# Experts as sorted token tiles, and four blocks as one stream of heads

## The reference

```
qp, kp = exp(q.W - |q|^2/2), exp(k.W - |k|^2/2)         # 16 heads of 64, 128 features
S_t = S_(t-1) + k_t v_t^T ;  a_t = (q_t.S_t) / (q_t.sum k + eps)     # causal linear attention
x1 = layernorm(x + a @ Wo)
x2 = layernorm(x1 + differential cross attention over the context)   # 32 half heads of 8
s = sigmoid(x2 @ gate_w.T)                               # 16 experts in 4 groups
best 2 groups, then best 4 experts of them; w = 2.5 * s / sum of the chosen s
out = layernorm(x2 + shared(x2) + sum_k w_k * expert_k(x2))
expert(x) = (silu(x @ gate.T) * (x @ up.T)) @ down.T     # 256 -> 128 -> 256
```

## Time and profile before

| | us |
|---|---|
| median of 3 runs | 1121.97 |
| span of the profiled execution (the time it has) | 1123.0 |
| TensorE busy | 957.9 (85%) |
| VectorE busy | 684.9 (61%) |
| ScalarE busy | 511.6 (46%) |
| GpSimd busy | 290.7 (26%) |
| moved by DMA | 81.72 MB, 73 GB/s |

### The profile page before, as it was taken

How to read it: one execution, slowest core, us unless ns; L and a number is a source line. 1 busy time by engine, 2 the same in 40 slices (tenths; PEclk the granted TensorE clock), 3 DMA queues, 4 the chain that set the end, 5 groups by cost and what they waited for, 6 DMA issues and landing times.

```text
span 1123.0 us, 20741 instructions
## 1 busy us (share of the span) xinstructions
PE 957.9 (85%) x7032; PEld 664.1 (59%) x7032; DVE 684.9 (61%) x1834; ACT 511.6 (46%) x910; POOL 290.7 (26%) x297
## 2 busy tenths in 40 slices
PE   4899976789998899789998899789998899764896
PEld 1477765347777566347777665347777675333453
DVE  5576643455556866654556766655556767855756
ACT  4676620367772323357773223347773223253221
POOL 2211100024440112125441112214441122133222
PEclk9999977799998999899998999989999999866998
DMA  5655652211113123201113123311114122300231
GB/s 158 214 163 160 129 123 80 67 29 30 39 29 104 57 71 93 80 19 39 30 39 104 52 64 89 89 26 37 32 29 113 43 65 87 94 1 1 73 106 52
DMA packets 79134, 81.72 MB, mean 73 GB/s; under 512 B 17968, under 2 KB 62640, under 8 KB 79024
## 3 DMA queue, kind: packets, MB, share of 16 engines
q1 hardware_dynamic: 79024, 80.31, 26.4%
HBM read 48.62 MB, written 11.73 MB: 54 GB/s over the span
## 4 chain that ended last, share of the span: by engine, by line
PE 64%; ACT 14%; DVE 11%; issue 6%; DMA 2%; POOL 1%; SPq 1%; DVEq 0%; ACTq 0%; POOLq 0%
PE ps_a L1171 18%; PE ps_xo L1171 6%; PE ps_o L1198 5%; PE ps_o L1197 4%; PE ps_o L1171 3%; PE ps_f L1171 3%; PE ps_turn L1171 3%; PE ps_att L1313 3%; PE ps_st L1326 3%; PE ps_st L1171 2%; PE ps_att L1171 2%; ACT square L690 2%; PE ps_f L1302 2%; ACT qk L685 2%; ACT qk L684 2%
## 5 line engine op out<-in xcount | busy, mean ns | idle before, releaser
L605 POOL TENSOR_TENSOR hT<-square,qk 128x512 f16<-128x512 f32 x64 | 74.0, 1157 | 370.8 <-DVE qk L935 370.8
L639 POOL TENSOR_TENSOR hT<-ffn_mem,hT 128x512 f16<-128x512 f32 x68 | 83.5, 1229 | 315.6 <-ACT hT L773 315.6
L933 DVE SCALAR_TENSOR_TENSOR hT<-ps_a,qk 128x512 f16<-128x512 f32 x64 | 44.3, 692 | 169.9 <-ACT square L690 165.5
L619 POOL TENSOR_TENSOR prob<-ffn_mem,prob 128x512 f16<-128x512 f32 x84 | 97.1, 1156 | 87.7 <-ACT ffn_mem L731 87.7
L1171 PE MATMUL ps_a<-turned,ffn_mem 128*128 128x512 f16 x432 | 101.3, 385 | 0.5 <-DMA ffn_mem<-ffn_split 0.5
L1198 PE MATMUL ps_o<-run,qf 128*128 128x65 f32 x480 | 93.8, 277 | 0.0
L1197 PE MATMUL ps_o<-v,att 128*128 128x65 f32 x480 | 90.4, 270 | 0.0
L1197 PEld LDWEIGHTS ps_o<-v,att 128*128 128x128 f32 x480 | 77.8, 194 | 7.7 <-issue 0.3
L1302 PE MATMUL ps_f<-qk,w_feat_high 128*128 128x512 f16 x128 | 48.9, 382 | 34.9 <-ACT qf L712 25.6
L1171 PE MATMUL ps_a<-w_v,x_split 128*128 128x512 f16 x192 | 54.4, 439 | 25.4 <-DVE w_v L823 12.9
L1326 PEld LDWEIGHTS ps_st<-v,kt 128*128 128x128 f32 x512 | 70.1, 200 | 8.3 <-ACT kt L708 0.3
(11 more groups left out here) (235 smaller groups left out, 2162.9 us busy)
## 6 DMA issues: line engine op xcount, KB each, us to landing
ffn_mem<-ffn_split SPq DMA_DIRECT2D x68, 256.0 KB, 3.0
qk<-hT SPq DMA_DIRECT2D x128, 128.0 KB, 2.4
ffn_mem<-ffn_split SPq DMA_DIRECT2D x68, 128.0 KB, 2.5
ffn_mem<-ffn_w SPq DMA_DIRECT2D x17, 384.0 KB, 4.3
ffn_split<-ffn_mem SPq DMA_DIRECT2D x17, 384.0 KB, 2.5
xv<-xv_blocks SPq DMA_DIRECT2D x4, 816.0 KB, 5.9
xq<-xq_hl SPq DMA_DIRECT2D x48, 64.0 KB, 2.0
x_stage<-xT SPq DMA_DIRECT2D x5, 512.0 KB, 5.1
```

The costliest lines, as they stand in the source:

```text
L605: pool.tensor_tensor(low_parts[:, n % 2, 1, :], square[:, n % 2, :], qk[:, n % 2, n // 2 % 2, 0, 1, :], ALU.subtract).then_inc(p_sql.sem, 1)
L619: pool.tensor_tensor(prob[:, n % RING, 1, :], prob_full[:, n % 2, :], prob[:, n % RING, 0, :], ALU.subtract).then_inc(pr_low[n % 2].sem, 1)
L639: pool.tensor_tensor(hT[:, e % 3, 1, :], hid[:, e % 2, :], hT[:, e % 3, 0, :], ALU.subtract).then_inc(h_low.sem, 1)
L933: dve.scalar_tensor_tensor(low_parts[:, n % 2, 0, :], bank[:, :], 1 / W_SCALE, pair[:, 0, 0, :], ALU.mult, ALU.subtract).then_inc(p_low.se ...
```

## The change

- The program is one list of jobs, `schedule()`, that every engine walks without a loop. The heads of the four blocks follow one another (64 steps and four to drain), with the values of block b in the steps around its first head, and the chain of each block (output projection to token sorting) spread over the steps 4 to 20 after its attention.
- Each job that writes PSUM takes the next of eight banks in rotation.
- In even blocks the running state starts from zero, and the first chunk's product with it is left out; in odd blocks the state after the last chunk is not made.
- Only the shared expert is dense. For the others a prefix sum over the chosen experts gives every token and choice a row in a DRAM buffer sorted by expert; 16 indirect DMAs of 128 rows on GpSimd's queue write a block's rows. Blocks 0 to 2 are group 0, block 3 is group 1. Tiles of 128 rows (64 and 32 of them, two to a pair) are read from a row number held in a register, multiplied with the weights of the expert held in another register (all weights are in SBUF, in the memory of the attention weights), and stored. For each block 16 indirect DMAs fetch the rows back, and VectorE accumulates them with their weights (`combine`).
- SyncE writes 128 rows of zeros behind the last row of each expert (`table`).
- Silu is made from Tanh. A probability tile has one exponential; VectorE makes its fp16 copy.
- Setup weights have staging memory of their own.

The job lists, whole:

```diff
-            with pe.Fori(0, NBLK - 1) as i:
-                shared(i + 1, i)
-                ffn(i, i + 1)
+GROUPS = ((0, 1, 2), (3,))
+NGRP = len(GROUPS)
+GROUP_OF = {b: g for g, blocks in enumerate(GROUPS) for b in blocks}
+TOKENS = [len(blocks) * TB for blocks in GROUPS]
+REGION = [t + P for t in TOKENS]
+TILES = [2 * -(-(t * TOPK // P + NE - 1) // 2) for t in TOKENS]
+PAIRS_OF = [t // 2 for t in TILES]
+SPARE = [t - n * TOPK // P for t, n in zip(TILES, TOKENS)]
+ROWS = [NE * r + s * P for r, s in zip(REGION, SPARE)]
+TILE_BASE = [sum(TILES[:g]) for g in range(NGRP)]
+PAIR_BASE = [sum(PAIRS_OF[:g]) for g in range(NGRP)]
+XG = 3
+YG = 4
...
+def attention_jobs(t):
+    jobs = []
+    def add(kind, g, per):
+        if 0 <= g < NBLK * per:
+            jobs.append((kind, g // per, g % per))
+    if t + 2 >= 2:
+        add("project", t + 2, H)
+    add("turn keys", t - 1, H)
+    add("q features", t, H)
+    add("state", t - 2, H)
+    add("attend", t - 1, H)
+    if t % 2 == 1:
+        add("turn output", (t - 5) // 2, PAIRS)
+    add("k features", t, H)
+    add("output", t - 3, H)
+    for b in range(1, NBLK):
+        for c in range(NT):
+            if t == H * b - NT + c:
+                jobs.insert(3, ("values", b, 2 * c))
+            if t == H * b + NT - 1 + c:
+                jobs.insert(3, ("values", b, 2 * c + 1))
+    return jobs
+def weighs(b, last_chunk):
+    return [("weigh", b, m) for g in range(NG) if last_chunk == GC * g + GC - 1 for m in (2 * g, 2 * g + 1)]
+def chain_jobs(b, s):
+    def several(kind, ns):
+        return [(kind, b, n) for n in ns]
+    jobs = []
+    if s == 4:
+        jobs += several("project out", range(NT)) + [("norm1", b, 0)]
+    if s == 5:
+        jobs += several("turn stream", range(2))
+    if s == 6:
+        jobs += several("queries", range(KD))
+    if s in (7, 8, 9):
+        jobs += several("scores", {7: range(0, 6), 8: range(6, 19), 9: range(19, 32)}[s])
+    if s == 10:
+        jobs += several("turn maxima", [0])
+    if 11 <= s <= 15:
+        for n in range(6 * (s - 11), min(6 * (s - 10), CHUNKS) + 0):
+            jobs += [("probs", b, n)]
+            if n >= 3:
+                jobs += weighs(b, n - 3)
+        if s == 15:
+            jobs += weighs(b, CHUNKS - 1) + [("norm2", b, 0)]
+    if s == 16:
+        jobs += several("turn cross", range(2))
+    if s == 17:
+        jobs += several("gate", [0]) + several("route", [0]) + several("shared up", range(2)) + several("route", [1])
+    if s == 18:
+        jobs += several("route", [2]) + several("shared down", range(2))
+    if s == 19:
+        jobs += several("route", [3]) + several("prefix", [0])
+    if s == 20:
+        jobs += several("dispatch", [0]) + several("keep", [0])
+        if b == GROUPS[GROUP_OF[b]][-1]:
+            jobs += [("table", GROUP_OF[b], 0)]
+    return jobs
+def merged(main, extra):
+    out, done = [], 0
+    for i, job in enumerate(main):
+        out.append(job)
+        upto = len(extra) * (i + 1) // len(main)
+        out += extra[done:upto]
+        done = upto
+    return out + extra[done:]
...
+def tile_jobs(grp, s):
+    n, jobs = PAIRS_OF[grp], []
+    for kind, k in (("rows in", s + 2), ("tile turn", s), ("tile up", s - 1), ("tile turn back", s - 2),
+                    ("tile down", s - 3), ("rows out", s - 3)):
+        if 0 <= k < n:
+            jobs.append((kind, grp, k))
+    return jobs
...
+def schedule():
+    jobs = [("values", 0, n) for n in range(2 * NT)]
+    jobs += [("project", 0, 0), ("project", 0, 1), ("context", 0, 0)]
+    last = H * NBLK + 4
+    for t in range(last):
+        extra = []
+        for b in range(NBLK):
+            if t == H * b + 1 and b + 1 < NBLK:
+                extra.append(("load x", b + 1, 0))
+            if b and t == H * b - 6:
+                extra.append(("split x", b, 0))
+            if t == H * b + 13:
+                extra.append(("load stream", b, 0))
+            if t == H * b + 1 + H and b % BLK_PER_BATCH == 0:
+                extra.append(("load context", b, 0))
+            extra += chain_jobs(b, t - H * (b + 1))
+        jobs += merged(attention_jobs(t), extra)
+        if t < EXPERTS + 1:
+            jobs.append(("setup", 0, t))
+        if t == H * NBLK - 8:
+            jobs.append(("experts", 0, 0))
+        if t == H * NBLK - 1:
+            jobs.append(("experts", 0, 1))
+    b = NBLK - 1
+    chain = []
+    for s in range(4, 21):
+        chain.append(chain_jobs(b, s))
+    jobs += chain_jobs(NBLK - 2, last - H * (NBLK - 1))
+    jobs += chain[0]
+    gaps = {1: chain[1], 2: chain[2]}
+    scores = [j for part in chain[3:6] for j in part]
+    for i in range(7):
+        gaps[4 + i] = scores[5 * i:5 * i + 5]
+    gaps[12] = chain[6]
+    weigh = [j for part in chain[7:12] for j in part]
+    per = -(-len(weigh) // 12)
+    for i in range(12):
+        gaps[14 + i] = weigh[per * i:per * (i + 1)]
+    for i, part in enumerate(chain[12:]):
+        gaps[28 + i] = part
+    for s in range(-2, PAIRS_OF[0] + 4):
+        jobs += merged(tile_jobs(0, s) or [("none", 0, 0)], gaps.pop(s, []))
+    for s in sorted(gaps):
+        jobs += gaps[s]
+    first = [(bb, c) for bb in GROUPS[0] for c in range(NT)]
+    for s in range(-2, PAIRS_OF[1] + 4):
+        extra = []
+        if 0 <= s < len(first):
+            bb, c = first[s]
+            if c == 0:
+                extra.append(("load sum", bb, 0))
+            extra.append(("gather", bb, c))
+        if 1 <= s <= len(first):
+            bb, c = first[s - 1]
+            extra.append(("combine", bb, c))
+            if c == NT - 1:
+                extra.append(("norm3", bb, 0))
+        jobs += merged(tile_jobs(1, s) or [("none", 0, 0)], extra)
+    for bb in GROUPS[-1]:
+        if bb != b:
+            jobs.append(("load sum", bb, 0))
+        for c in range(NT):
+            jobs.append(("gather", bb, c))
+        for c in range(NT):
+            jobs.append(("combine", bb, c))
+        jobs.append(("norm3", bb, 0))
+    return jobs
...
```

The bodies that matter, in the order SyncE, GpSimd, ScalarE, VectorE, TensorE:

```diff
-ps_a = [psum("ps_a0"), psum("ps_a1")]
+banks = [stack.enter_context(nc.psum_tensor(f"ps{i}", [P, 512], F32)) for i in range(8)]
+KEY_BANK, VALUE_BANK = 6, 7
+BANK = {}
+turn = 0
+early = True
+for kind, b, n in SCHEDULE:
+    if kind == "q features" and (b, n) == (0, 4):
+        early = False
+    if kind in ON_PSUM and job_bank(kind, b, n) not in BANK:
+        if early and turn % 8 in (KEY_BANK, VALUE_BANK):
+            turn += 8 - turn % 8
+        BANK[job_bank(kind, b, n)] = turn % 8
+        turn += 1
...
+        elif kind == "table":
+            sp.wait_ge(*table_ready(0, b + 1))
+            for e in range(NE):
+                r = sp.value_load(end_i[0:1, b, e:e + 1], min_val=0, max_val=ROWS[b] - P)
+                sp.dma_start(rows_in[b][bass.ds(r, P), :], zero_row[:, :]).then_inc(ends_zeroed[b].sem, 16)
+        elif kind == "rows in":
+            i = pair_id(b, n)
+            if n == 0:
+                for bb in GROUPS[b]:
+                    sp.wait_ge(*scattered[bb](0, NT * TOPK))
+                sp.wait_ge(*ends_zeroed[b](0, NE))
...
+            if i >= XG:
+                sp.wait_ge(*t_turned(0, i - XG + 1))
+            for j in range(2):
+                t = TILE_BASE[b] + 2 * n + j
+                r = sp.value_load(row_i[0:1, t:t + 1], min_val=0, max_val=ROWS[b] - P)
+                sp.dma_start(xg[:, i % XG, j, :], rows_in[b][bass.ds(r, P), :]
+                             ).then_inc(xg_loaded[i % XG].sem, 16)
+        elif kind == "rows out":
+            i = pair_id(b, n)
+            sp.wait_ge(*t_kept(0, i + 1))
+            tiles = rows_out[b][2 * P * n:2 * P * (n + 1), :].rearrange("(j p) d -> p j d", p=P)
+            sp.dma_start(tiles, yb[:, i % XG, :, :]).then_inc(yb_stored[i % XG].sem, 16)
...
+        elif kind == "dispatch":
+            pool.wait_ge(*slots_ready(b, 1))
+            for j in range(NT * TOPK):
+                pool.indirect_dma_start(
+                    rows_in[GROUP_OF[b]], bass.IndirectOffsetOnAxis(ap=slot_i[:, b, j:j + 1], axis=0),
+                    stream[:, b % 2, j // TOPK, :], None).then_inc(scattered[b].sem, 16)
+        elif kind == "gather":
+            i = NT * b + n
+            if n == 0 and b == GROUPS[GROUP_OF[b]][0]:
+                upto_pair = PAIR_BASE[GROUP_OF[b]] + PAIRS_OF[GROUP_OF[b]]
+                pool.wait_ge(*back_ready(0, GROUP_OF[b] + 1))
+                for r in range(XG):
+                    pool.wait_ge(*yb_stored[r](len(range(r, upto_pair, XG)), 0))
+            if i >= YG:
+                pool.wait_ge(*combined(0, i - YG + 1))
+            for k in range(TOPK):
+                j = TOPK * n + k
+                pool.indirect_dma_start(
+                    yg[:, i % YG, k, :], None, rows_out[GROUP_OF[b]],
+                    bass.IndirectOffsetOnAxis(ap=back_i[:, b, j:j + 1], axis=0)
+                ).then_inc(yg_loaded[i % YG].sem, 16)
...
```

(118 more changed lines are left out.)

1717 lines of the change are left out of this document (849 added, 868 removed).

## The result

The changed kernel takes 1180.72 us (median of 4, 1175.2 to 1183.2) against 1125.78 beside it: ratio 1.0489, 95% interval 1.0441 to 1.0537. It is 5% slower; I had forecast 1024 and faster with a chance of 0.80. The same kernel, run again later, took 1112.63 (1107.4 to 1116.1) against 1126.06, ratio 0.9855 (0.9795 to 0.9916): 1.5% faster. The kernel before takes 1125 to 1127 on every chip. So part of the result does not belong to the kernel. I call the sets of runs by letters: A (the result), B, C, D and E. Each was made on one chip, B to E on four different ones; the chip of A is not known and can be one of the four. For short I say "chip A" and so on, but what else may have differed between the sets I can't see.

A forecast was written before the change was run, and what follows sets the result against it. TensorE was taken as the bound nearly everywhere. The stream ends at 144 + 484 + 27 + 30 = 685, first tile 721, group 0 done 892, group 1 starts 906; 906 + 122 = 1028, less 4: 1024 us, range 950 to 1135.

The forecast's parts named there:

- Waits on top: Steps 16 to 63: engine waits added to 484 us of work, idle share 5.5% kept from the old head stretch, 27 us.
- SyncE's placing of queries: Before each block's first score: 12 x 0.64 + 2.0 = 9.7 us, against one step of about 8, counted inside the 27.
- That slack covers 1.2 per issue, not 2.4.: GpSimd's queue in the stream: a block's 16 indirect DMA issues, 19 us, fit before the features two steps on.
- Rival 4: An indirect DMA costs GpSimd 2.4 us instead of 1.2: 138 us more, 1162 and slower; chance 0.13.
- Before step 16: Kernel start to step 16: ten steps at 6.6 and four values pairs, less earlier savings; step 16 starts at 144 us.
- Into the tiles: Stream's end to first tile: slots 4.5, table 11, indirect DMAs 18, first rows 2.5; 36 us, reaching 721.
- Register reads: Group 0's tile pairs: TensorE reads two registers per pair at 0.6 us each, half hidden under VectorE; 18 us.
- Rival 3: Tile pairs: register reads cost a DMA landing each, 2.0 us, a pair 6.6; total 1114; chance 0.09.
- rival 1: Tile phases run at the low clock, a pair 5.2 us, group 0 217 instead of 171; total about 1084; chance 0.10.
- Group 1 to the end: Second tile group, combines, last gathers, norm and store: 72 + 13 + 6 + 31 = 122 us, less 4 for overlap.
- Rival 5: In-order VectorE still costs 5.6 us per norm, slots and route, four times in three blocks: +67, 1091; chance 0.06.
- rival 2: Everything overlaps: no stream waits (27) and free register reads (18), total about 975; chance 0.15.

The follow-up runs named there:

- all edits: Changed kernel plus all gaining edits: dispatches spread, chain later, zeros in pieces, table split, GpSimd pauses, later combine, two exponentials: 1059.3 us, ratio 0.9407 to the kernel before.
- the pauses: Three small GpSimd subtractions behind every four indirect DMAs, against the kernel with dispatches spread, scores later, zeros in pieces and table split: 1076.0 us, from 1094.0.
- D (18.1 us steps with a row of 16): Changed kernel with three small GpSimd subtractions behind every four gathers and behind each dispatch's sixteenth indirect DMA: 1128.1 us, ratio 1.0022 to the kernel before.
- ten stretches: Changed kernel with ten stretches of 240 TensorE matmuls behind its end, beside differing rows of DMAs: no gap in any; 26.4 us is the undisturbed time.

## Why the prediction was wrong, point by point

By E's run the sign was right and the size was not (1112.6 for 1024); by A's both were wrong. On E the forecast is short by 90 us of the profiled 1114.3: 23 before step 16, 43 in the stream, 5, 14 and 5 in the three stages behind it. On A the gaps beside the rows come on top.

- **The step that failed is "Waits on top"**, 27 us as a share carried over from the kernel before; I had named a stream that ends after 740 as proof against me, and the last head's output came at 775. Measured on A: 582.5 - 484 = 98.5. Two dispatch steps are 29.5 of it (31.7 and 33.8 for 18.0; nothing on E), three scores steps 34.5 by the edit that moved them, the rest 34.5. With all edits the stretch is 512.1 where I said 511 (by blocks 166, 176 and 170; without the waits I had 155, 168 and 161). So the sum by the longer of TensorE and VectorE fits, with 8 to 11 us a block on top of it. But that is another kernel, with VectorE's copies gone, so that the equal totals are in part luck.
- **"SyncE's placing of queries ... has one step of about 8 before the first score; inside my 27."** I had worked out 9.7 us of need against 8 of cover and then let it go. TensorE idled 9.1 us in each block and ran at the lower level for 5.2 behind it.
- **"That slack covers 1.2 per issue, not 2.4."** I had set 1.2 for an issue; it took 1.27 from start to start (0.97 of work, 0.30 between), and the slack held. Rival 4 is refuted in its mechanism, though its 1162 and its sign came nearest. What I left out is that a row of them can stop TensorE: no row of before could show it, but an operation that the trace has never seen wants a bound for its neighbours too, not only for its own duration.
- **Before step 16**, 144 for 169.0: the spare tiles' zeros, 4 MB in SyncE's queue at step 6, stand in the diff and in no term of my sum; spreading them gave 15.6. The other 9 stay open; step 14 (14.0 us on A, 3.0 of them TensorE's wait for a low part's move) holds part of them.
- **Into the tiles:** from the last head's output to the first tile 51.9 for my 36, with 28.7 of it TensorE waiting for a DMA, as forecast (20 to 30). Routing still ran there: the slots were ready 13.1 us behind that output, where I had set 4.5. SyncE's sixteen took 21.8 us here and 24.0 before group 1 for my 20; splitting them gave 13.7 over both groups. **Before group 1** TensorE stood 26.9 us, where I had set 14: here too it waits for the rows behind SyncE's sixteen.
- **Register reads**, 18: measured 19.2, in part luck: I had half of every read hidden, and nearly all of the 19.2 is in group 0 (19.9 there, 0.7 in group 1). Rival 3 (2.0 each) is refuted: 0.69 for a read and one matmul bare, 0.18 beyond six matmuls.
- **The clock.** I priced all at the full level and held the low one for the tile phases (rival 1). It was 0.83 and 0.73 there, but 0.90 to 0.93 in the stream too, behind each wait. Rival 1 fails in its mechanism: on A the clock was 1.00 from 866 to 940 us, through the middle of group 0, although each pair has six transposes to eighteen matmuls; it was low behind the waits at both ends. TensorE is busy 861.1, 101 above my 760 (835.7 on E, 823.7 in the last version).
- **VectorE's copy**, 0.42: 0.77 in the kernel. Beside GpSimd's subtractions it took 1.33 by itself, which explains it well; undoing the copies was worth 8.5 and 4.2 us in two kernels.
- **Group 1 to the end**, 118: 147.1 on A and 123.2 on E, so the forecast of this stage was good. That the rows of gathers are its excess on A is borne out by the pauses, which gave 18.0 on C. The end without TensorE, 31: 34.9.
- **Rival 5** (5.6 us per norm, slots and route) showed as 3.1 to 3.3 ahead of the cross turn once a block, 5.2 in the drain steps; rival 2 (no waits) not at all.

## What to carry to other kernels

Where the working of one job gives need and cover (9.7 against 8), the difference is a term of the sum, once for each block, and in a diff every DMA has its bytes and its place in the queue, the setup's too. When a step shows gaps inside one accumulation group, look at what GpSimd issues beside it. Before an effect is put down to an edit, run the unchanged kernel again beside it: here the same kernel differed by 6% between two sets of runs, more than any single edit gave.

## What the runs showed of the hardware that I had not expected

- On chips A, B and C, indirect DMAs of 128 rows in an unbroken row hold up TensorE from about 8 to 11 us after the first one on: nothing at 6, 1.5 us at 8, 8.4 at 12, 13 to 15 at 16, for 240 matmuls of 26.4; with scatter and gather, rows of 1024 and 512 bytes, in a loop and unrolled; not with plain DMAs from GpSimd or SyncE, nor with a subtraction of 1.3 us behind every four. On D (18.1 us steps with a row of 16) and E (ten stretches) nothing of this shows; that the chip makes the difference is likely, not shown.
- A VectorE copy from fp32 to fp16 in SBUF takes 0.34 us alone and 1.33 beside GpSimd's subtractions.
- A register read on TensorE costs about 0.5 to 0.6 us bare (0.69 with its one matmul, most of them at the lower clock) and 0.18 where six matmuls stand before the next.
- Two DMAs of 2 MB ahead of small ones in one queue made TensorE wait 11.8 us.
